# Eight-head attention on Trainium2: the probability-value product turned round, with softmax sums copied to every partition of a head

## The reference, cut to what matters

```
x = x + L3_xattn(layernorm(x), ctx)            # x: (16, 256, 256)

q = layernorm(x) @ Wq ; k, v = split(layernorm(ctx) @ Wkv)     # inner width 8 * 64 = 512
sim  = einsum('bhid,bhjd->bhij', q, k) * 64 ** -0.5
attn = softmax(sim, axis=-1)
out  = einsum('bhij,bhjd->bhid', attn, v)
x    = x + out @ Wout + bout
```

## Time and profile before

| | us |
|---|---|
| median of 3 runs (lowest, highest) | 3641.53 (3633.49, 3645.52) |
| the profiled execution | 3635.24 |
| span of its instructions | 3633.5 |
| PE busy in the span | 2925.8 |
| DVE busy | 2018.9 |
| ACT busy | 1661.6 |
| PE busy from 3100 to 3200 us, inside layer a4 | 96.93 |
| DVE busy in the same 100 us | 50.20 |

### The profile page before, as it was taken

The page is one execution under the profiler, slowest core; times in us unless marked ns, Lnnn a source line. Parts: engine busy times, 40 slices in busy tenths (PEclk is TensorE's granted clock), DMA queues, the critical chain, the costliest instruction groups (busy, mean ns, idle before and its releaser), DMA issues. The chain is left out here.

```text
span 3633.5 us, 71573 instructions
## 1 busy us (share of the span) xinstructions
PE 2925.8 (81%) x26488; PEld 1935.1 (53%) x26488; DVE 2018.9 (56%) x4658; ACT 1661.6 (46%) x3102; POOL 813.2 (22%) x772
## 2 busy tenths in 40 slices
PE   4888676888789999999699968996159859999932
PEld 2544353444346666666455536664158836666621
DVE  3777554777555444433477746776624335455456
ACT  2777332666534444444267635665235423333300
POOL 4332005555000000000222233430420143233000
PEclk8999796999879999999799979997579969999965
DMA  3221002111124000000111101110423323333101
GB/s 102 67 71 55 13 1 74 60 62 61 46 58 131 1 1 1 1 1 1 41 55 54 52 26 45 39 45 11 146 95 93 110 64 79 79 77 77 41 5 46
DMA packets 195045, 189.56 MB, mean 52 GB/s; under 512 B 25924, under 2 KB 173272, under 8 KB 194552
## 3 DMA queue, kind: packets, MB, share of 16 engines
q1 hardware_dynamic: 188568, 168.24, 15.0%
q0 software_dynamic: 6144, 16.79, 1.6%
HBM read 66.70 MB, written 41.42 MB: 30 GB/s over the span
## 5 line engine op out<-in xcount | busy, mean ns | idle before, releaser
L1438 DVE TENSOR_TENSOR f1H<-f1HF,f1H 128x512 bf16<-128x512 f32 x256 | 176.6, 692 | 396.6 <-ACT f1H L1283 396.6
L1216 PE MATMUL ps<-f1xT,f1w 128*128 128x512 bf16 x1536 | 378.7, 383 | 5.9 <-ACT f1H L1283 5.9
L1238 PE MATMUL ps<-f1w,f1H 128*128 128x256 bf16 x3072 | 377.8, 273 | 0.0
L1238 PEld LDWEIGHTS ps<-f1w,f1H 128*128 128x128 bf16 x3072 | 301.2, 98 | 90.0 <-issue 1.1
L1280 ACT ACTIVATE f1HF<-ps 128x512 f32<-128x512 f32 x256 | 152.8, 597 | 333.9 <-PE ps L1216 333.8
L1216 PEld LDWEIGHTS ps<-f1xT,f1w 128*128 128x128 bf16 x1536 | 148.3, 98 | 151.0 <-issue 16.9
L781 DVE TENSOR_REDUCE a0NM<-ps 128x2 f32<-128x512 f32 x256 | 166.7, 684 | 62.9 <-PE ps L480 62.5
L781 DVE TENSOR_REDUCE a1NM<-ps 128x2 f32<-128x512 f32 x256 | 166.3, 685 | 44.6 <-PE ps L480 44.1
L781 DVE TENSOR_REDUCE a2NM<-ps 128x2 f32<-128x512 f32 x256 | 165.7, 684 | 27.2 <-PE ps L480 25.9
L778 DVE TENSOR_REDUCE a3NM<-ps 128x1 f32<-128x128 f32 (+1 forms) x512 | 149.2, 348 | 43.2 <-PE ps L502 39.8
L664 ACT ACTIVATE a1PT<-ps 128x512 f32<-128x512 f32 x256 | 144.3, 595 | 51.1 <-PE ps L491 49.5
(11 more groups left out here) (563 smaller groups left out, 7085.6 us busy)
## 6 DMA issues: line engine op xcount, KB each, us to landing
a4KS<-a4KH SPq DMA_DIRECT2D x96, 128.0 KB
a4QS<-a4QH SPq DMA_DIRECT2D x96, 128.0 KB, 2.8
slots<-zeros SPq DMA_DIRECT2D x1, 9984.0 KB, 31.5
f2XS<-slots SPq DMA_DIRECT2D x39, 256.0 KB, 3.0
results<-f2XS SPq DMA_DIRECT2D x39, 256.0 KB, 2.1
f1WF<-in_f_w SPq DMA_DIRECT2D x32, 256.0 KB, 2.7
f2WF<-in_f_w SPq DMA_DIRECT2D x16, 512.0 KB, 4.8
a0KS<-a0KH SPq DMA_DIRECT2D x96, 64.0 KB
```

Source lines behind the costliest of these rows:

```text
L1216: m = nc.tensor.matmul(ps[:, (u * NCH + i) % 2, :], w1[:, x, kt, i * P:i * P + P], xT[:, half, y, kt, :], start=(j == 0), stop=(j == len(t ...
L1238: m = nc.tensor.matmul(out, H[:, (u * NCH + i) % HR, x, t * P:t * P + P], w2[:, y, i, :], start=first, stop=(f == YC - 1 and j == 2 and no ...
L1438: nc.vector.tensor_tensor(H[:, (u * NCH + i) % HR, 1, :], HF[:, (u * NCH + i) % 2, :], H[:, (u * NCH + i) % HR, 0, :], SUB).then_inc(S["h_ ...
```

## The change

In wide mode only:

- `pv` is turned round. V (128x64, fp32) is stationary and the probabilities move, 256 columns. The two heads of a step go to the two column halves of the array (`tile_position=(0, 64*j)`), and so to the two halves of the PSUM partitions: the context comes out with channels in the partitions and queries in the free dimension. A second set of products has a 128x64 block of ones as its stationary operand, so that the softmax sum of each query stands in all 64 partitions of its head, in the other half of the same bank.
- DVE takes the reciprocal of that 128x256 block of sums (`RL`), multiplies (`OF`), ACT copies to bf16 (the high part), and DVE subtracts for the low part (`low`), in four pieces of 128x256 instead of two of 128x512. The low part of a piece is taken behind the next piece's product; that of the last piece in a new step `olo`.
- The transposes `o2T` are gone, and with them their two turns of the PSUM banks. `oT` has two buffers.
- The buffer `GB` of gathered expert rows becomes a view of the last eight tiles of `Y`.

```diff
@@ attention
-    W = 80 if wide else 32
-    VW = DH + 1 if wide else 32
+    W = 32
+    VW = DH if wide else 32
+    OC = 4 if wide else NB
@@ slots
-        if proj:
+        if wide:
+            put(4, "olo", "p", 3)
+        elif proj:
             for i in range(NB):
                 put(5 + i, "o2T", "p", i)
@@ buffers
-        O = sb("O", [P, 2, C], F32)
-        oT = sb("oT", [P, 2, CK, SEQ], BF16)
+        OF = sb("OF", [P, 2, SEQ], F32) if wide else None
+        RL = sb("RL", [P, 2, SEQ], F32) if wide else None
+        O = None if wide else sb("O", [P, 2, C], F32)
+        oTs = sb("oT", [P, 2 if wide else 1, 2, CK, SEQ], BF16)
-        GB = sb("GB", [P, 4, 2, D], F32) if gather else None
+        GB = Y[:, TILES - 8:TILES, :].rearrange("p (r k) d -> p r k d", k=2)
@@ PE, step pv
+                        for part in range(2 if wide else 0):
+                            for kt in range(2):
+                                for j in range(HS):
+                                    h = i * HS + j
+                                    w = g["onesf"][:, 0:DH] if part else VA[:, u % 3, kt, h, :]
+                                    m = nc.tensor.matmul(misc[DH * j:DH * j + DH, part * SEQ:part * SEQ + SEQ], w,
+                                                         PT[:, h, kt * SEQ:kt * SEQ + SEQ], start=(kt == 0), stop=(kt == 1),
+                                                         tile_position=(0, DH * j))
-                                if wide:
-                                    a = (t * HS + j) * W
-                                    for kt in range(2):
-                                        m = nc.tensor.matmul(misc[:, a:a + VW],
-                                                             PT[:, slot, kt * SEQ + t * P:kt * SEQ + t * P + P],
-                                                             VA[:, u % 3, kt, h, :], start=(kt == 0), stop=(kt == 1))
...
@@ ACT, a new part of step pv
+                    elif name == "pv":
+                        act.wait_ge(S["o_ready"].sem, S["o_ready"].at(u, i + 1))
+                        act.wait_ge(S["y_ps"].sem, S["y_ps"].at(u - 2, 1))
+                        nc.scalar.activation(oTs[:, u % 2, 0, i, :], OF[:, i % 2, :], ACT.Copy).then_inc(S["o2_hi"].sem, 1)
@@ DVE, step pv
+                def low(u, i):
+                    dve.wait_ge(S["o2_hi"].sem, S["o2_hi"].at(u, i + 1))
+                    nc.vector.tensor_tensor(oTs[:, u % 2, 1, i, :], OF[:, i % 2, :], oTs[:, u % 2, 0, i, :], SUB
+                                            ).then_inc(S["o2_lo"].sem, 1)
+                    elif name == "pv" and wide:
+                        dve.wait_ge(S["pv_ps"].sem, S["pv_ps"].at(u, i + 1))
+                        nc.vector.reciprocal(RL[:, i % 2, :], misc[:, SEQ:2 * SEQ]).then_inc(S["recip"].sem, 1)
+                        dve.wait_ge(S["recip"].sem, S["recip"].at(u, i + 1))
+                        dve.wait_ge(S["o2_hi"].sem, S["o2_hi"].at(u, i + 1 - 2))
+                        nc.vector.tensor_tensor(OF[:, i % 2, :], misc[:, 0:SEQ], RL[:, i % 2, :], MUL
+                                                ).then_inc(S["o_ready"].sem, 1)
+                        if i:
+                            low(u, i - 1)
+                    elif name == "olo":
+                        low(u, i)
```

More of the change, by code:

```diff
@@ L101, in attention @@
                k_lo=NB, v_ps=NB, v_sb=NB, s_ps=NH, s_max=NH, mT_ps=2, m_hi=2, m_lo=2, st_ps=NH, p_ready=NH,
-               pv_ps=4, pv_sb=4, oT_ps=NO, recip=NO, o_ready=NO, o2T_ps=NB, o2_hi=NB, o2_lo=NB,
+               pv_ps=4, pv_sb=4, oT_ps=NO, recip=NO, o_ready=NO, o2T_ps=NB, o2_hi=OC, o2_lo=OC,
                q_moved=NQD, k_moved=NQD + (2 if mask else 0), m_moved=2 * NMD)
@@ L596, in _ @@
                         take(before)
-                        for t in range(2):
+                        for part in range(2 if wide else 0):
[6 more added lines that the diff above has]
+                                                         tile_position=(0, DH * j))
+                        for t in range(0 if wide else 2):
                             q0 = P if causal and t == 1 else 0
@@ L601, in _ @@
                                 slot = order(h) % 8
-                                if wide:
-                                    a = (t * HS + j) * W
-                                    for kt in range(2):
-                                        m = nc.tensor.matmul(misc[:, a:a + VW],
-                                                             PT[:, slot, kt * SEQ + t * P:kt * SEQ + t * P + P],
-                                                             VA[:, u % 3, kt, h, :], start=(kt == 0), stop=(kt == 1))
[L608 to L612, removed]
+                                m = nc.tensor.matmul(misc[32 * j:32 * j + 32, q0:SEQ], VA[:, u % 3, t, h, :],
+                                                     PT[:, slot, t * SEQ:t * SEQ + SEQ - q0],
+                                                     start=(t == 0), stop=(t == 1 or causal),
+                                                     skip_group_check=bool(causal), tile_position=(0, 32 * j))
                         m.then_inc(S["pv_ps"].sem, 1)
@@ L631, in _ @@
                     elif name == "y" and proj:
-                        pe.wait_ge(S["o2_hi"].sem, S["o2_hi"].at(u, NB))
-                        pe.wait_ge(S["o2_lo"].sem, S["o2_lo"].at(u, NB))
+                        pe.wait_ge(S["o2_hi"].sem, S["o2_hi"].at(u, OC))
+                        pe.wait_ge(S["o2_lo"].sem, S["o2_lo"].at(u, OC))
+                        oT = oTs[:, u % 2 if wide else 0]
                         take(before)
@@ L720, in _ @@
                         nc.scalar.activation(OS[:, i, :], misc[:, 0:SEQ], ACT.Copy).then_inc(S["pv_sb"].sem, 1)
+                    elif name == "pv":
+                        act.wait_ge(S["o_ready"].sem, S["o_ready"].at(u, i + 1))
+                        act.wait_ge(S["y_ps"].sem, S["y_ps"].at(u - 2, 1))
+                        nc.scalar.activation(oTs[:, u % 2, 0, i, :], OF[:, i % 2, :], ACT.Copy).then_inc(S["o2_hi"].sem, 1)
                     elif name == "o2T":
+                        oT = oTs[:, 0]
                         act.wait_ge(S["o2T_ps"].sem, S["o2T_ps"].at(u, i + 1))
@@ L865, in _ @@
                                                 ).then_inc(S["m_lo"].sem, 1)
[L866 to L870, removed]
+                    elif name == "pv" and wide:
[9 more added lines that the diff above has]
+                        low(u, i)
+                    elif name == "oT":
+                        dve.wait_ge(S["oT_ps"].sem, S["oT_ps"].at(u, i + 1))
                         ng = NH // NO
@@ L914, in signal_used @@
     proj, mask, self_att = cfg.get("proj"), cfg.get("mask"), cfg.get("self")
-    if n in ("o2T_ps", "o2_hi", "o2_lo", "y_ps"):
+    if n == "o2T_ps":
+        return bool(proj) and not wide
+    if n in ("o2_hi", "o2_lo", "y_ps"):
         return bool(proj)
```

## The result

The changed kernel takes 3648.74 us (median of 11 runs, 3643.67 to 3657.90), the kernel before 3638.79 us (11 runs beside them, 3631.57 to 3656.58): the ratio is 1.0030, with a 95% interval of 1.0016 to 1.0044. So it is slower by 0.3%, some 11 us: little, but the interval leaves out no change. The forecast was no change.

A forecast was written before the change was run, and what follows sets the result against it. PE was taken to bound layer a4; transposes and idle -2.23, pv +0.44, entry +0.10, new waits +0.72 and +0.77 gave -0.20 us an item, -3.2 over 16, so 3638.3 us, no change. Range 3614 to 3659; the forecast's own 3629 to 3649.

The forecast's parts named there:

- What bounds: Layer a4: PE bounds, busy 96.93 of 100 us; other engines matter only where PE waits for them.
- What goes: On PE: transposes free 1.19 us and idle before pv and v 1.04, together 2.23 us less an item.
- pv on PE: Each turned pv step takes 1.88 us instead of 1.77; four steps add 0.44 us an item.
- rival 3: In pv, column halves don't run side by side: +6.8 us an item, +109 us, 3750; chance 0.08.
- The entry: At each pv step the array changes shape twice: +0.10 us an item taken, bounded by 0 and 0.28.
- The reciprocal: On DVE, 256 elements in a partition take 1.75 us, with 1.59 and 1.82 as ends.
- rival 2: On DVE, a longer reciprocal of 2.22 us: +0.84 us an item, +13 us, 3655; chance 0.17.
- The two new waits: PE waits 0.72 us at maxT for head 7's maximum, 0.77 at pv step 2 for head 5's exponential.
- The sum for one item: Layer a4, per item: -2.23 + 0.44 + 0.10 + 0.72 + 0.77 = -0.20 us.
- 16 items, -3.2 us: Whole layer a4: the -0.20 us an item holds for all 16 items, -3.2 us in all.
- the two old waits: PE's v waits for DVE's context product (13 times, 9.7 us), pv for k's low part (13 times, 3.2 us).
- Rival 1: Both new waits in a4 are hidden: -1.69 us an item, -27 us, 3614.5; chance 0.22.

The follow-up runs named there:

- the kernel with both late moves: Changed kernel with ACT's context copy behind the next head's exponential and the maxima's transposes of heads 4 to 7 behind pv step 3: 3620.33 us, ratio 0.9963.
- Late copy: Changed kernel with only ACT's order changed, the bf16 copy of a context piece behind the next head's exponential: 3629.96 us, ratio 0.9990.
- late transposes: Changed kernel with only the transposes of the maxima of heads 4 to 7 moved behind pv step 3: 3642.90 us, ratio 1.0021.
- The first experiment: Changed kernel with the reciprocal of the sums replaced by a plain copy for the last three batch items only: 3635.49 us, ratio 1.0003.
- the slowed kernel of before: Kernel before with a further 128x256 reciprocal of a constant on DVE at each pv step, and gathered rows in Y: 3656.70 us, ratio 1.0058.

## Why the prediction was wrong, step by step

- **What bounds: right.** PE, at 97 in 100 before and after; other engines matter by where PE waits.
- **What goes: right.** No transposes, no idle time before v and pv step 0.
- **pv on PE: right in its size.** 1.88 us from row to row (3203.05 to 3204.93), as worked out from 32-column strips; two strips of 64 columns do run side by side, and rival 3 has fallen. The entry was undersized: maxT before pv takes 0.37 us instead of 0.28, and xT and q before pv 0.09 more likewise, so 0.27 us an item for the 0.10 taken, just under the upper bound of 0.28. Where no wait stands ahead of pv step 2, as in the kernel with both late moves, that step has 0.10 of it too: 0.37, above the bound.
- **The reciprocal: right.** 1.757 us for the 1.75 that was taken from the trace's slope. The rule of the Trainium skill (page "VectorE: DVE Perf Modes", section "Walkthrough: the 8-slice pipeline in each mode") read as eight cycles an element gave 2.2 us; the measurement decides for about 6.3 ns an element, and rival 2 has fallen.
- **The two new waits: right in place, cause and size.** 0.73 and 0.71 us for 0.72 and 0.77. They are the only ones in the middle. Late copy and late transposes take away one each.
- **The sum for one item: right within 0.2 us.** -0.20 forecast, +0.01 measured; the entry accounts for 0.17 of it.
- **"16 items, -3.2 us": the step that failed.** I multiplied the period of the middle by all items. Twelve periods are of that length; the last three have another bound. There PE's work no longer covers the chain through DVE and ACT: in the last two each pv step starts some 3.3 us after the end of the one before, with only about 1 us of products between them. Against the kernel before the three lost 1.4, 4.8 and 5.3 us, 11.5 together; the sum had put a cost of their own at nothing, without a reason. The first experiment puts the loss there: 10 us by the medians, 15.8 by the trace, come back when only those twelve reciprocals are cheap. A part of it is the clock, which was not in the prediction at all. Rows 3 held the sign: the two old waits stood there 13 times each, and the sum counted them 16 times.
- **Rival 1** gave 3614.5 us for waits that are hidden. The hiding did not come by itself. It comes by order, with the reciprocal as long as it is: with both orders mended the period is 30.61 us, where that rival's sum gives 30.25; 0.27 us of the difference is the entry (0.37 for 0.10).

The range held the time, but not by its reasons: of the chance of 0.28 for slower, 0.20 was given to a long reciprocal and to strips that don't overlap, and neither happened. The signs that the prediction named, one wait missing, a third wait, a period outside 31.2 to 32.4 us, all looked at the middle, and none of them came. The forecast's own range should also have begun at 3627 and not at 3629 us, by its own terms (0.32 + 0.10 + 0.30 us, 16 times, under 3638.3).

## What to carry to other kernels

A pipeline over items has a middle and an end: work out a change for both, since an engine that is hidden in the middle sets the pace once the bound engine runs out of other work. On engines that walk one list in order, put an instruction that waits behind every one that doesn't need what it waits for; here two moves in the table were worth 1.34 us of 31.95 an item, shortened the last periods besides, and turned a loss of 0.3% into a gain of 0.4%. Before making a result copied to all partitions, price the copying on both sides: here the products with ones cost 3.2 us an item, more than the transposes and the idle time that went, and the reciprocal of 256 elements in the place of 4 took ten times as long.

## What was new about the hardware

- A reciprocal on DVE takes about 6.3 ns for each further element of a partition in fp32: 353 ns for 128x32, 1757 for 128x256 out of PSUM, and 1749 and 1752 out of SBUF, where a product of the same size takes 425. Where the input lies makes under 10 ns of difference.
- fp32 products with 64 stationary columns run two at a time in the two column halves: 16 instructions of 256 columns in 1.88 us, where the prediction's sum for one at a time gave 3.63. Going into such a step costs about 0.09 us over going into one that uses the whole array (0.37 for 0.28 behind maxT, 0.54 for 0.45 behind xT).
- At the end of the layer, where PE waits often, the granted clock went from 2.4 to 1.2 GHz in some kernels and not in others: 0.66 over 5 us and 0.64 over the last 24 us in the changed kernel, 0.73 over the last 19 us in the kernel before, 0.50 and 0.51 over 15 us in the slowed kernel of before, 1.00 throughout with the cheap last reciprocals. A pv step of 1.88 us took 3.21 there.
